# Attention B with keys on partitions: no turned probabilities, the maxima subtracted in PSUM, 64-row products

## The reference

```
q = (resid @ Wq)   32 heads of 16        k, v = resid @ Wk, resid @ Wv   8 heads of 16
q, k = rope(q), rope(k)
att = einsum("bhgqd,bhkd->bhgqk", q, k) / sqrt(16)      4 query heads share a key head
att = where(causal, att, -inf)
probs = softmax(att, axis=-1)
out = (probs @ v) @ Wo
```

## Time and profile before

| | |
|---|---|
| median of 3 runs | 1111.4 us (1109.72 to 1111.72) |
| the profiled execution | 1111.0 us, span 1108.9 us |
| busy share of the span | PE 93%, DVE 77%, ACT 62%, POOL 54% |
| mean granted PE clock | 0.978 of full |
| attention B, first score product to last context turn | 822.6 to 1029.4 us |

### The profile page before, as it was taken

How to read it: one execution, slowest core, us unless ns; L and a number is a source line. 1 busy time by engine, 2 the same in 40 slices (tenths; PEclk the granted TensorE clock), 3 DMA queues, 4 the chain that set the end, 5 groups by cost and what they waited for, 6 DMA issues and landing times.

```text
span 1108.9 us, 21316 instructions
## 1 busy us (share of the span) xinstructions
PE 1025.7 (93%) x7267; PEld 592.8 (53%) x7267; DVE 856.9 (77%) x1853; ACT 689.7 (62%) x1522; POOL 602.5 (54%) x680
## 2 busy tenths in 40 slices
PE   3679999999999999999999997879879999998998
PEld 1345555555555555555555553445546666665554
DVE  5777777877777877778878886778768999997654
ACT  2366666766676666666666654433778999997221
POOL 3787786777777687677768731456541121211111
PEclk9899999999999999999999998989989999999999
DMA  8065454555635635634854653000000000000002
GB/s 282 24 176 148 116 141 124 158 99 129 174 79 147 177 84 121 186 105 90 197 122 86 149 143 72 1 1 1 1 1 1 1 1 1 1 1 1 1 1 76
DMA packets 179746, 94.89 MB, mean 86 GB/s; under 512 B 168016, under 2 KB 168528, under 8 KB 175056
## 3 DMA queue, kind: packets, MB, share of 16 engines
q1 hardware_dynamic: 169872, 49.11, 20.9%
q10 hardware_dynamic: 9792, 44.59, 12.1%
HBM read 49.64 MB, written 2.10 MB: 47 GB/s over the span
## 4 chain that ended last, share of the span: by engine, by line
PE 66%; issue 14%; DVE 8%; POOL 7%; ACT 4%; DMA 1%; POOLq 1%; SPq 0%; ACTq 0%; DVEq 0%
PE bank L959 15%; PE bank L960 15%; PE bank L961 15%; PE bank L1046 3%; PE bank L1048 3%; PE bank L1047 3%; POOL shift L635 3%; PE bank L1067 3%; PE bank L1069 3%; PE bank L1068 3%; DVE xn L1403 2%; PE bank L1049 1%; PE bank L969 1%; POOL rq L620 1%; PE bank L1165 1%
## 5 line engine op out<-in xcount | busy, mean ns | idle before, releaser
L481 POOL TENSOR_TENSOR rt<-rt 128x512 f32<-128x512 f32 x80 | 101.1, 1267 | 149.8 <-DVE rt L1495 149.8
L1535 DVE SCALAR_TENSOR_TENSOR bw_hi<-bank,rden,bw_hi 128x128 f16<-128x128 f32 (+3 forms) x256 | 123.3, 544 | 60.5 <-ACT bw_hi L729 60.5
L709 ACT ACTIVATE prob<-bank,shift,c_score_b 128x128 f32<-128x128 f32 (+3 forms) x256 | 145.9, 631 | 14.4 <-POOL shift L635 13.9
L698 ACT ACTIVATE bank<-bank,shift,c_score 128x128 f32<-128x128 f32 (+3 forms) x256 | 147.3, 605 | 2.1
L729 ACT ACTIVATE bw_hi<-bank,rden 128x128 f16<-128x128 f32 (+3 forms) x256 | 114.2, 529 | 30.4 <-DVE rden L1528 30.4
L1509 DVE TENSOR_REDUCE smax<-bank 128x1 f32<-128x512 f32 (+3 forms) x256 | 109.2, 481 | 26.4 <-PE bank L1049 24.9
L635 POOL TENSOR_TENSOR shift<-smax,c_score_b 128x1 f32<-128x1 f32 (+1 forms) x192 | 37.0, 193 | 158.1 <-DVE smax L1519 152.3
L1519 DVE TENSOR_REDUCE smax<-bank 128x1 f32<-128x128 f32 (+3 forms) x256 | 108.6, 483 | 13.3 <-PE bank L1276 12.4
L693 ACT ACTIVATE shift<-smax,c_score 128x4 f32<-128x4 f32 x64 | 19.0, 297 | 153.6 <-DVE smax L1509 153.6
L959 PE MATMUL bank<-xt,wq_hi 128*128 128x512 f16 x256 | 98.6, 385 | 2.0 <-DVE rt L1495 1.8
L1306 PE MATMUL bank<-ident,prob 128*128 128x128 f32 x640 | 98.4, 285 | 0.4 <-DVE ptb L1846 0.4
(11 more groups left out here) (229 smaller groups left out, 2854.4 us busy)
## 6 DMA issues: line engine op xcount, KB each, us to landing
qcode<-in_q_codes ACTq DMA_DIRECT2D x8, 1024.0 KB, 4.9
qscale<-in_q_scales ACTq DMA_DIRECT2D x8, 1024.0 KB, 7.5
ocode<-in_o_codes ACTq DMA_DIRECT2D x7, 1024.0 KB, 4.9
oscale<-in_o_scales ACTq DMA_DIRECT2D x7, 1024.0 KB, 8.6
kvcode<-in_k_codes ACTq DMA_DIRECT2D x8, 256.0 KB, 7.4
kvcode<-in_v_codes ACTq DMA_DIRECT2D x8, 256.0 KB, 8.1
kvscale<-in_k_scales ACTq DMA_DIRECT2D x8, 256.0 KB, 8.6
kvscale<-in_v_scales ACTq DMA_DIRECT2D x8, 256.0 KB, 8.9
```

The lines of the kernel that those rows point to most:

```text
L698: act.activation(a_rows(i, s), a_rows(i, s), ACT.Exp, bias=shift[:, s % 2, c:c + 1], scale=c_score[:, 0:1], accum_out=bank[3][:, SUMS_AT + ...
L709: act.activation(prob[:, i2, S_OFF[i]:S_OFF[i] + w], bank[bk][:, o:o + w], ACT.Exp, bias=shift[:, i2, c:c + 1], scale=score[:, 0:1]).then_ ...
L1535: dve.scalar_tensor_tensor(out=p_row[:, s % 2, LO_AT[i]:LO_AT[i] + P_STEP * i + 1:P_STEP], in0=turned_back(i, s), scalar=rden[:, s % 2, c: ...
```

## The change

A set (q = 2j + batch) is now the unit, and attention B runs in 16 sets with everything written out; nothing outside B changes but what feeds it.

- kt_b keeps each key head once, copied into both halves of the rows, with no zeroes. The two heads of a pair are taken as two 64-row products, one on rows 0 to 63 and one on 64 to 127, in different banks.
- Row scores (queries on partitions, b_scores) are made for their maxima alone, two sets ahead, in banks 0 and 1 or 2 and 3. VectorE reads both heads' banks in one instruction (b_max).
- POOL splits the set's maxima in three bfloat16 terms (b_split), PE turns them, four 128-row products (b_turn_max), and VectorE copies them out (b_max_out).
- Key scores (keys on partitions, b_keys) are made in five steps of two banks, out of the three banks 4, 6 and 7; a 64-row product with selectors subtracts the maxima in PSUM, and the diagonal mask is added as four products of 64 columns. ScalarE takes exps of 512 columns straight into pt, with no bias (b_exps); there are no probabilities to turn and to copy.
- Masks are products of 64 rows and 64 columns of constants in sel, which a new load of 128x1024 float32 on SyncE's queue brings and POOL casts in place of the zeroing of kt_b.
- The V products, the context's copy and turn, and the division stay, in the order given in the loop over q on PE.

```diff
+SETS = 2 * KV_HEADS
+B_STEPS = [(0, 0, 3), (0, 0, 2), (0, 0, 1), (0, 1, 3)]
+for _q in range(SETS):
+  B_STEPS += [(_q, 1, 2), (_q, 1, 1)]
+  B_STEPS += [(_q + 1, 0, 3), (_q + 1, 0, 2)] if _q + 1 < SETS else []
+  B_STEPS += [(_q, "max", 0)]
+  B_STEPS += [(_q + 1, 0, 1), (_q + 1, 1, 3)] if _q + 1 < SETS else []
+STEP_AT = {step: i for i, step in enumerate(B_STEPS)}
+KEY_BANKS = (4, 6, 7)
...
-    prob = sb("prob", [P, 2, TRI], F32)
+    smax_b = sb("smax_b", [P, 2, 2, 2, ST], F32)
+    low_b = sb("low_b", [P, 2, 2, 2, ST], F32)
+    m_stack = sb("m_stack", [P, ST, P], BF16)
+    m_turned = sb("m_turned", [P, 2, S], BF16)
+    sel_f = sb("sel_f", [P, B_CONSTS], F32)
+    sel = sb("sel", [P, B_CONSTS], BF16)
...
-    kt_b = sb("kt_b", [P, KV_HEADS, 2, TOK], F16)
+    kt_b = sb("kt_b", [P, KV_HEADS, TOK], F16)
...
-    pt_home = [ptb[:, i] for i in range(5)] + [xt_32[:, i * TRI:(i + 1) * TRI] for i in range(3)]
+    pt = sb("pt", [P, 8, TRI], F32)
...
+  sp.dma_start(sel_f[:], t_in["sel"]).then_inc(d_sel, 16)
...
-  pool.memset(kt_b[:].rearrange("p h f n -> p (h f n)").bitcast(F32), 0.0).then_inc(zeros_done, 1)
+  pool.memset(m_stack[:].rearrange("p i n -> p (i n)").bitcast(F32), 0.0).then_inc(zeros_done, 1)
+  pool.wait_ge(d_sel, 16)
+  pool.tensor_tensor(sel[:], sel_f[:], one[:].broadcast_to([P, B_CONSTS]), ALU.mult).then_inc(zeros_done, 1)
...
-        pool.tensor_tensor(shift[:, s % 2, c0:c1], smax[:, s % 2, c0:c1],
-                  c_score_b[:, 1:2].broadcast_to([P, c1 - c0]), ALU.mult).then_inc(bshift, 1)
+  def b_split(q):
+    m = smax_b[:, q % 2].rearrange("p c f i -> p i f c")
+    low = low_b[:].rearrange("p k c f i -> p k i f c")
+    term = m_stack[:].rearrange("p i (f n) -> p i f n", f=2)[:, :, :, 0:6].rearrange(
+      "p i f (c r) -> p i f c r", r=3)
+    ones = one[:].unsqueeze(1).unsqueeze(1).broadcast_to([P, ST, 2, 2])
+    pool.wait_ge(bs_read, STEP_AT[q, 1, 1] + 1)
+    if q == 0:
+      pool.wait_ge(zeros_done, 1)
+    else:
+      pool.wait_ge(bs_ps, STEP_AT[q - 1, "max", 0] + 1)
+    pool.tensor_tensor(term[..., 0], m, ones, ALU.mult).then_inc(bsplit, 1)
+    pool.wait_ge(bsplit, 4 * q + 1)
+    pool.tensor_tensor(low[:, 0], m, term[..., 0], ALU.subtract).then_inc(bsplit, 1)
+    pool.wait_ge(bsplit, 4 * q + 2)
+    pool.tensor_tensor(term[..., 1], low[:, 0], ones, ALU.mult).then_inc(bsplit, 1)
+    pool.wait_ge(bsplit, 4 * q + 3)
+    pool.tensor_tensor(low[:, 1], low[:, 0], term[..., 1], ALU.subtract).then_inc(bsplit, 1)
+    pool.wait_ge(bsplit, 4 * q + 4)
+    pool.tensor_tensor(term[..., 2], low[:, 1], ones, ALU.mult).then_inc(bsplit_done, 1)
+  for q in range(SETS):
+    b_split(q)
...
+  def b_exps(q, which):
+    home = GROUP * (q % 2)
+    for i in which:
+      act.wait_ge(bk_ps, LOADS * q + i + 1)
+      ps = key_bank(LOADS * q + i)
+      if i < 8:
+        f, part, c = i % 2, i // 2 % 2, i // 4
+        act.activation(pt[:, home + 2 * c + f, part * S:(part + 1) * S], ps, ACT.Exp,
+                scale=c_score_b[:, 0:1]).then_inc(bexp, 1)
+      else:
+        f = i - 8
+        act.activation(pt[:, home + f:home + f + 3:2, 2 * S:TRI], ps.rearrange("p (c n) -> p c n", c=2),
+                ACT.Exp, scale=c_score_b[:, 0:1]).then_inc(bexp, 1)
...
+  for q in range(SETS + 2):
+    if q < SETS:
+      b_exps(q, range(8))
+    if 1 <= q <= SETS:
+      b_ctx_out(q - 1)
+    if q < SETS:
+      b_exps(q, range(8, LOADS))
...
+  def b_mask(kind, out_at):
+    for n in range(2):
+      w = B_MASK_W + (2 * kind + n) * P
+      m = B_MASK + (2 * kind + n) * P // 2
+      for f in range(2):
+        rows = slice(f * P // 2, (f + 1) * P // 2)
+        mm = pe.matmul(out_at[f][:, n * P // 2:(n + 1) * P // 2], sel[rows, w:w + P],
+                sel[rows, m:m + P // 2], start=False, stop=(n == 1))
+    return mm
+  def b_scores(q, c, i):
+    j, b = q // 2, q % 2
+    at = STEP_AT[q, c, i]
+    if at >= 2:
+      pe.wait_ge(bs_read, at - 1)
+    tiles = ((2, P), (0, 0)) if i == 2 else ((i, 0),)
+    for ti, o in tiles:
+      for f in range(2):
+        rows = slice(f * P // 2, (f + 1) * P // 2)
+        pe.matmul(bank[2 * (at % 2) + f][:, o:o + (ti + 1) * P],
+             qt_b[rows, 2 * j + c, b * S + ti * P:b * S + (ti + 1) * P],
+             kt_b[rows, j, b * S:b * S + (ti + 1) * P], start=True, stop=False)
+      mm = b_mask(0, [bank[2 * (at % 2) + f][:, o + ti * P:o + (ti + 1) * P] for f in range(2)])
     mm.then_inc(bs_ps, 1)
+  def b_turn_max(q):
+    at = STEP_AT[q, "max", 0]
+    pe.wait_ge(bs_read, at - 1)
+    pe.wait_ge(bsplit_done, q + 1)
+    for i in range(ST):
+      mm = pe.matmul(bank[2 * (at % 2)][:, i * P:(i + 1) * P], m_stack[:, i], ident_b[:], start=True,
+              stop=True)
+    mm.then_inc(bs_ps, 1)
+  def key_scores(q, c, f, kt, out_ap):
+    j, b = q // 2, q % 2
+    rows = slice(f * P // 2, (f + 1) * P // 2)
+    pe.matmul(out_ap, kt_b[rows, j, b * S + kt * P:b * S + (kt + 1) * P],
+         qt_b[rows, 2 * j + c, b * S + kt * P:(b + 1) * S], start=True, stop=False)
+  def less_max(q, c, f, kt, out_ap):
+    rows = slice(f * P // 2, (f + 1) * P // 2)
+    pe.matmul(out_ap, sel[rows, c * P:(c + 1) * P], m_turned[rows, q % 2, kt * P:S], start=False, stop=False)
+  def b_keys(q, step):
+    load = LOADS * q + 2 * step
+    heads = range(2)
+    out_at = [key_bank(load + f) for f in heads]
+    if load >= 2:
+      pe.wait_ge(bexp, load - 1)
+    if step == 4:
+      pieces = ((0, 2, 0), (1, 2, 2 * P))
+    else:
+      c = step // 2
+      pieces = ((c, 1, 0), (c, 3, 3 * P)) if step % 2 else ((c, 0, 0),)
+    for c, kt, o in pieces:
+      for f in heads:
+        key_scores(q, c, f, kt, out_at[f][:, o:o + S - kt * P])
+      if step == 0:
+        pe.wait_ge(bs_read, STEP_AT[q, "max", 0] + 1)
+      for f in heads:
+        less_max(q, c, f, kt, out_at[f][:, o:o + S - kt * P])
+      mm = b_mask(1, [out_at[f][:, o:o + P] for f in heads])
+    mm.then_inc(bk_ps, 2)
...
-      mm = pe.transpose(bank[B_PT_BANK[piece]][:, o:o + P],
-               prob[:, i2, S_OFF[i] + kt * P:S_OFF[i] + (kt + 1) * P], ident[:])
...
+  for q in range(-1, SETS + 2):
+    here = 0 <= q < SETS
+    ahead = q + 1 < SETS
+    ahead2 = q + 2 < SETS
+    back = 1 <= q <= SETS
+    if here:
+      b_keys(q, 0)
+    if ahead:
+      b_scores(q + 1, 1, 2)
+    if here:
+      b_keys(q, 1)
+    if ahead:
+      b_scores(q + 1, 1, 1)
+    if q >= 2:
+      b_ctx_turn(q - 2)
+    if ahead2:
+      b_scores(q + 2, 0, 3)
+    if here:
+      b_keys(q, 2)
+    if back:
+      b_pv(q - 1, 0)
+    if ahead2:
+      b_scores(q + 2, 0, 2)
+    if ahead:
+      b_turn_max(q + 1)
+    if here:
+      b_keys(q, 3)
+    if ahead2:
+      b_scores(q + 2, 0, 1)
+    if back:
+      for kt in range(1, ST):
+        b_pv(q - 1, kt)
+    if here:
+      b_keys(q, 4)
+    if ahead2:
+      b_scores(q + 2, 1, 3)
...
+  def b_max(q, c, i):
+    at = STEP_AT[q, c, i]
+    two = banks[:, 2 * (at % 2):2 * (at % 2) + 2]
+    dve.wait_ge(bs_ps, at + 1)
+    if i == 3 and c == 0 and q >= 2:
+      dve.wait_ge(bsplit_done, q - 1)
+    if i == 2:
+      dve.tensor_reduce(smax_b[:, q % 2, c, :, 2], two[:, :, P:4 * P], AX, ALU.max)
+      last = dve.tensor_reduce(smax_b[:, q % 2, c, :, 0], two[:, :, 0:P], AX, ALU.max)
+    else:
+      last = dve.tensor_reduce(smax_b[:, q % 2, c, :, i], two[:, :, 0:(i + 1) * P], AX, ALU.max)
+    last.then_inc(bs_read, 1)
+  def b_max_out(q):
+    at = STEP_AT[q, "max", 0]
+    dve.wait_ge(bs_ps, at + 1)
+    dve.tensor_copy(m_turned[:, q % 2], bank[2 * (at % 2)]).then_inc(bs_read, 1)
```

More of the change, by code:

```diff
@@ L166, in sem @@
             return ctx.enter_context(nc.semaphore(name))
-        bank = [ctx.enter_context(nc.psum_tensor(f"bank{i}", [P, 512], F32)) for i in range(8)]
+        banks = ctx.enter_context(nc.psum_tensor("bank", [P, 8, 512], F32))
+        bank = [banks[:, i] for i in range(8)]
         x = sb("x", [P, NT, D], F32)
@@ L305, in build, with key_bank @@
         stage.close()
[L308 to L310 removed]
+        pt = sb("pt", [P, 8, TRI], F32)
         ctx_t = sb("ctx_t", [P, S], F32)
         rden_b = sb("rden_b", [P, ST, GROUP], F32)
[L314 to L316 removed]
+        def key_bank(load):
+            return bank[KEY_BANKS[load % 3]]
         def a_bank(i, s):
@@ L1838, in b_ctx @@
                                   ALU.mult).then_inc(bctx, 1)
-            def b_turned(n, s):
-                banks = B_PT_BANK
-                dve.wait_ge(bpt_ps, 3 * n + 2)
-                dve.tensor_copy(pt_home[s][:, S:2 * S], bank[banks[1]][:]).then_inc(bpt_dve, 1)
-                dve.wait_ge(bpt_ps, 3 * n + 3)
-                dve.tensor_copy(pt_home[s][:, 2 * S:TRI], bank[banks[2]][:, 0:TRI - 2 * S]).then_inc(bpt_dve, 1)
-            def b_group(j, first):
-                for s in range(8):
-                    n = 8 * j + s
-                    if s % 4 == 1 and not first:
-                        b_ctx(2 * j - 2 + s // 4, j - 1, s // 4)
-                    row_max(n, s % 2, bs_ps, bsmax)
```

(14 more changed lines are left out.)

154 lines of the change are left out of this document (41 added, 113 removed).

## The result

The changed kernel takes **1071.6 us** (median of four runs, 1069.69 to 1072.27), the kernel before 1111.6 beside it (1109.72 to 1113.73): ratio 0.9643, 95% interval 0.9629 to 0.9657, about 40 us less. The profiled execution took 1071.7 us, span 1069.8. Forecast were 1091 and a range from 1076 to 1113: the direction is right, and the gain is twice the one forecast and outside the range. One of the four executions of a later run, the one with the memset put back, took 1195.4 us at a granted clock of 0.841 where every other has 0.970 or more; that run is compared by its other three.

The account below looks back on a forecast made before the run. The old loop has ScalarE as its fullest link; after the change PE's in-order path sets 10.9 us a set instead of 11.8. 1111.0 - 13.4 (attention B) - 7 (before it) = 1090.6, forecast 1091; 1083 to 1099 (47%), 1076 to 1113 (80%).

Parts of the forecast that it names:

- the TensorE part: TensorE's work for one set of attention B: products and shape changes sum to 9.4 us, 10.9 with waits.
- The waits: TensorE idle before two key steps for exps (0.66, 0.53) and one row step for VectorE's read (0.35): together 1.5 a set.
- the slow start: At the start of attention B, 2.0 us given because PE is little used beforehand, granted clock 0.66.
- Exps without a bias: ScalarE in attention B: ten exps of 512 columns a set, each lasting 0.70 and following at 0.61.
- VectorE's wide reads across two banks: VectorE's maxima in attention B: 1.02 ns a column plus 0.09 fixed per read, 6.0 us a set.
- Memset: Before the stage: without kt_b's zeroing VectorE's xn is no longer held; 7 us saved, from 4 to 9.
- The load of the selectors: Last in SyncE's queue, 512 KB: priced at nothing, at most its own length, some 1.5 us.
- A: 64-row pairs in row and key scores don't run beside each other: 2.4 x 16 = 38 later, 1129; chance 8%.
- B: Small 64-row products start 0.055 apart, not 0.025: 1.9 us a set, 30 in all, 1121; chance 6%.
- C: A weight load waits for the product using the same rows: 2.8 us a set, 45 in all, 1136; chance 3%.
- D: Hand-overs at key steps and shape changes cost more: 0.4 + 0.3 a set, 11 in all, 1102; chance 20%.
- E: Less waiting, shape changes nearly free, full 9 before the stage: 10.2 a set, 1078; chance 13%.

Follow-up runs that it names:

- the new order: The changed kernel with the same TensorE instructions reordered within a set, V products spread behind key steps 0 to 3 to cover all three waits: 1052.5 us, ratio 0.9470.
- the two runs with another order: The changed kernel with V products of key tiles 1 to 3 ahead of one row step, 1063.8 us; and with all three waits covered, 1052.5 us.

## Why the prediction was wrong in size

*The step that failed* is in the TensorE part: "I take the first, being nearest in kind", that is one stream plus 0.025 for a 64-row pair, with two streams as the other bound, and a mask group of four at 4 x 0.025. Both bounds lay above the truth: the second product of a pair costs nothing. A pair of 512 columns takes 0.22, and a mask group of four is two products of 64 columns long and costs 0.055, not 0.10; 0.10 is about what the four would take one after the other (4 x 64 columns at 0.216 for 512). Row scores then cost 1.08 + 8 x 0.055 = 1.52 (forecast 2.08), keys 2.16 + 0.44 = 2.60 (forecast 3.36); in the timeline of the new order, where no wait lies between, a set's row steps add up to 1.58 and its key steps to 2.67. TensorE's sum is 8.0 with that, 8.0 in the trace, 9.4 in the prediction. The column tiles that I went by share the rows on which data comes in and these pairs don't; that this is the reason no run shows.

*The waits* were at the right three places: 0.68, 0.61 and 0.57 for 0.66, 0.53 and 0.35. They grew to 1.87 from 1.5, which fits the shorter work between them (the row step between key steps 0 and 1 takes 0.34 and not 0.47): of 1.4 saved 0.35 was given back. That the stage is TensorE's queue with these waits in it, the two runs with another order show.

*The sum of the miss.* 15 sets x (10.9 - 9.87) = 15.5. The first key product was forecast for 833.4 and came at 831.59, 1.8 earlier: 0.9 from the memset, 2.0 from the slow start, which I had priced and which lay beside VectorE's reads (VectorE was busy 11.07 of the 12 us to 834, at a TensorE clock of 0.50), less the 1.1 by which the all-reduce ahead of it came later than in the trace before. That 1.1 says nothing of the change: in the traces of the runs the all-reduce stands anywhere from 721.2 to 725.6. From there to the end of the last turn the forecast had 175.4 and the trace 158.8, which is 1.1 more than the 15.5. Together 18.4 of 18.9.

*What held.* Exps without a bias: 684 ns, 0.70 forecast. VectorE's wide reads across two banks: one of 1024 and one of 512 columns take 1.82 together (new order, 905.98), 1.75 by the formula. Split: 0.23 an operation, hidden. Turned maxima 0.22, V 2.1 (2.20), changes of shape 0.11 (0.13). From the last key copy (824.1) to the first key product 7.5 us, 7.3 forecast. Memset 7.9, 7 forecast. The load of the selectors cost nothing that shows.

*The rivals.* A is out: pairs run beside each other. B is out: by its own words small products 0.055 apart; four of them take that. C is out: a product on the rows just in use follows at 0.22 with its weights hidden (909.75, 909.98). The rule of the Trainium skill (TensorE: Matmul & The Clock Gate, The mechanism) that a weight load overlaps only a product in other rows would, at the 0.1 a load that the prediction took, have put 0.1 behind each; this trace doesn't agree with it. D is out: the two waits for exps measured 0.68 and 0.61 for 0.66 and 0.53, and a change of shape 0.11. E had the right direction with 10.2 a set, from hand-overs, and stopped short for lack of the pairs.

## What to carry to other kernels

Where a cost in the engine that sets the pace stands in no row, ask also for its lowest possible value, here that the second product of a pair is free, and put it in the range with all the products that it touches. Here the better end was never priced, and the choice ran through 16 mask groups and all pairs. When work on the engine that sets the pace gets shorter, count again what stands between each product and the wait behind it: here the cheapest 19 us came afterwards, from spreading the V products over the places where TensorE waited. Products of half the rows are worth keeping in one shape: each change costs 0.1 us, more than a mask group does (0.055).

## What the hardware showed that was not expected

A product on the free half of the rows starts while up to four ahead of it in the queue are not done, so partners needn't be neighbours (three or four places apart: +0.3 us in all; eight: +24.7, of which some 4 lie ahead of the first copy of a context).

GpSimd's first tensor_tensor behind its all-reduce starts about 7 us after the instruction ahead of it has ended, whatever that is: 7.03 in the kernel before, 6.69 in the changed one, 7.13 with the memset back, 7.46 directly behind the all-reduce, and between 6.69 and 7.46 in all fourteen traces. Memsets start at once, and the same cast placed ahead of the all-reduce did too (0.44 after the memset's start, itself 0.47 long). What it waits for the traces don't say (they have "issue", and with the memset back a row of ScalarE), and no run here tells it.

A memset on GpSimd of 7 us holds a VectorE instruction of 0.54 us for its whole length, and eight memsets in a row hold it just as long (7.60).
